# Row sums taken from VectorE to GpSimd, and copies set ahead of exponentials in the last slots, in an attention block with top-32 masking

## The reference

```python
x = x + attn(layernorm(x)); x = x + ffn(layernorm(x))
# attn:
scores = q @ k.T * SCALE + (q @ rel_k[dist])           # dist clipped to +-64
threshold = top_k(scores, 32)[0][..., -1:]
attn = softmax(where(scores < threshold, -inf, scores))
for i in range(3):                                      # v_curr = v at first
    a_v = attn @ v_curr
    if i == 0: a_v = a_v + attn applied to rel_v[dist]
    v_curr = a_v
    res = res + sigmoid(alphas_raw)[i] * v_curr
out = res @ Wout.T + bout
# ffn: x @ base_w.T + base_b, plus 8 low-rank experts weighted by a softmax gate
```

## Time and profile before

| | |
|---|---|
| median of 3 runs | 712.65 us |
| profiled execution, own time | 714.7 us |
| its span, first to last instruction | 713.0 us |
| DVE, PE, ACT, POOL busy, share of span | 95%, 93%, 87%, 77% |
| granted TensorE clock, mean | 0.98 |
| a slot without batch work | 10.07 us, two heads of 5.03 |

### The profile page before, as it was taken

The page is one execution under the profiler, slowest core; times in us unless marked ns, Lnnn a source line. Parts: engine busy times, 40 slices in busy tenths (PEclk is TensorE's granted clock), DMA queues, the critical chain, the costliest instruction groups (busy, mean ns, idle before and its releaser), DMA issues.

```text
span 713.0 us, 20948 instructions
## 1 busy us (share of the span) xinstructions
PE 659.8 (93%) x5780; PEld 512.2 (72%) x5780; DVE 679.7 (95%) x2820; ACT 618.9 (87%) x1767; POOL 547.0 (77%) x978
## 2 busy tenths in 40 slices
PE   4368999999999999999999999999999999999796
PEld 3256777777777777777787777777777777777574
DVE  6899999999999999999999999999999999999953
ACT  4578899989999899989999899998999899998753
POOL 1588888778878788878877788778878788787840
PEclk9769999999999999999999999999999999999998
DMA  6745545544454454544454545454545454445212
GB/s 197 176 127 139 148 124 163 161 126 144 142 155 133 132 154 130 157 142 143 133 155 128 156 137 153 123 158 129 153 135 161 133 146 136 140 146 151 70 44 59
DMA packets 148338, 98.72 MB, mean 138 GB/s; under 512 B 10624, under 2 KB 147968, under 8 KB 148096
## 3 DMA queue, kind: packets, MB, share of 16 engines
q1 hardware_dynamic: 147920, 97.32, 47.2%
q10 hardware_dynamic: 304, 0.08, 0.0%
HBM read 45.59 MB, written 51.77 MB: 137 GB/s over the span
## 4 chain that ended last, share of the span: by engine, by line
DVE 77%; issue 9%; PE 5%; POOL 4%; DMA 2%; ACT 2%; SPq 0%; ACTq 0%; DVEq 0%; POOLq 0%
DVE top L722 40%; DVE work L728 34%; POOL s_sb L330 2%; DMA band_scratch<-zeros 1%; PE ps_p L947 1%; DVE rinv L709 1%; ACT a_sb L477 1%; PE ps_y L967 1%; POOL xn L372 1%; DMA band_scratch<-band 1%; DVE stats L744 0%; DMA skew<-band_scratch 0%; DVE xn L798 0%; DVE x_sb L737 0%; POOL wk L351 0%
## 5 line engine op out<-in xcount | busy, mean ns | idle before, releaser
L722 DVE MAX8 top<-work 128x8 f32<-128x256 f32 x768 | 285.6, 415 | 0.0
L728 DVE MATCH_REPLACE8 work<-top,work 128x256 f32<-128x256 f32 x512 | 206.5, 413 | 0.0
L330 POOL TENSOR_TENSOR s_sb<-s_sb,pen 128x512 f32<-128x512 f32 x127 | 161.9, 1275 | 39.5 <-ACT pen L467 38.3
L335 POOL TENSOR_SCALAR a_sb<-a_sb,rinv 128x256 f32<-128x256 f32 x254 | 118.7, 478 | 55.2 <-DVE rinv L709 54.8
L477 ACT ACTIVATE a_sb<-s_sb,nmax 128x256 f32<-128x256 f32 x256 | 128.2, 501 | 34.9 <-POOL s_sb L330 26.9
L467 ACT ACTIVATE pen<-s_sb,limit 128x256 f32<-128x256 f32 x254 | 116.4, 511 | 24.2 <-POOL limit L317 24.0
L305 POOL TENSOR_TENSOR s_sb<-s_sb,skew 128x384 f32<-128x384 f32 x128 | 128.3, 1003 | 4.3 <-DMA skew<-band_scratch 4.3
L947 PE MATMUL ps_p<-aT,rows 128*64 128x256 f32 x1024 | 125.3, 386 | 1.3 <-issue 0.5
L728 DVE MATCH_REPLACE8 work<-top,s_sb 128x256 f32<-128x256 f32 x256 | 103.2, 412 | 0.0
L722 DVE MAX8 top<-s_sb 128x8 f32<-128x256 f32 x256 | 94.7, 413 | 5.0 <-POOL s_sb L305 5.0
L855 PE MATMUL ps_a<-ident,a_sb 128*128 128x128 f32 x512 | 84.9, 289 | 13.8 <-POOL a_sb L335 13.8
(11 more groups left out here) (166 smaller groups left out, 1310.7 us busy)
## 6 DMA issues: line engine op xcount, KB each, us to landing
skew<-band_scratch SPq DMA_DIRECT2D x128, 192.0 KB, 2.7
diag_scratch<-a_sb SPq DMA_DIRECT2D x128, 192.0 KB, 3.1
band_scratch<-band SPq DMA_DIRECT2D x128, 191.0 KB, 3.7
diag<-diag_scratch SPq DMA_DIRECT2D x128, 128.0 KB, 2.2
wqkv<-in_wqkv SPq DMA_DIRECT2D x1, 1152.0 KB, 8.3
x_sb<-in_x SPq DMA_DIRECT2D x4, 256.0 KB, 4.7
wout<-in_wout SPq DMA_DIRECT2D x1, 512.0 KB, 5.7
out<-xn SPq DMA_DIRECT2D x1, 512.0 KB, 3.3
```

What stands on the lines that cost most here:

```text
L330: nc.gpsimd.tensor_tensor(s_sb[g % 4][:], s_sb[g % 4][:], pen[g % 2][:], ALU.subtract).then_inc(pen_added, 1)
L335: nc.gpsimd.tensor_scalar(a_sb[g % 3][:, t, :], a_sb[g % 3][:, t, :], rinv[g % 2][:, t:t + 1], 1.0, ALU.mult, ALU.mult).then_inc(normed, 1)
L722: nc.vector.max(m[:, t, 8 * n:8 * n + 8], src).then_inc(top_step, 1)
L728: nc.vector.match_replace(work[t][:, n % 2, :], m[:, t, 8 * n:8 * n + 8], src, LOW).then_inc(top_step, 1)
```

## The change

- `add_projection` leaves VectorE for the seven batches of the loop. ScalarE copies `ps_y` into a new SBUF tile `yp_sb` at the end of slots q = 11, 19, ..., 59 (`save_projection`), and GpSimd adds that tile to x in the next slot, between `negative_max(2q+1)` and `add_penalty(2q)`. The row moments stay on VectorE and move behind the second head of that slot. The last batch's add in the tail stays as it was.
- `second_normal` is split: one tile in slots with q % 8 = 7, the other in the slot after it. The transposes, layer products and their copies move one slot back with it.
- In slot 63 GpSimd's `add_penalty(126)` comes ahead of shift and normalised tiles.
- In slots 61, 62 and 63 (`late`) `save_diagonals` stands ahead of `exponent(2q-1)`, `save_aT(2q-1)` and `save_values` ahead of `exponent(2q)` on ScalarE, and TensorE does `diagonal_columns` ahead of `attention_columns(2q-2)`.
- In the tail VectorE does the last gate's small steps between and behind the sums of the first output group, and the second group's sums after them.

```diff
+        yp_sb = sb("yp_sb", [P, T, DIM])
...
-            def second_normal(b):
+            def second_shift(b):
                 i = slice(T * b, T * (b + 1))
                 pool.wait_ge(rstd2_done, b + 1)
                 nc.gpsimd.tensor_tensor(shift[:, i], shift[:, i], rstd[:, i], ALU.mult).then_inc(shift_done, 1)
+
+            def second_normal(b, t):
+                i = T * b + t
                 pool.wait_ge(shift_done, b + 1)
...
+                nc.gpsimd.tensor_scalar(yn[:, i, :], y_sb[:, i, :], rstd[:, i:i + 1], shift[:, i:i + 1], ALU.mult,
+                                        ALU.add).then_inc(yn_done, 1)
...
                 if b >= 0 and q % NP == 7:
-                    second_normal(b)
+                    second_shift(b)
+                    second_normal(b, 0)
+                if b >= 1 and q % NP == 0:
+                    second_normal(b - 1, 1)
+
+            def add_projection(b):
+                i = slice(T * b, T * (b + 1))
+                pool.wait_ge(yp_saved, b + 1)
+                nc.gpsimd.tensor_tensor(y_sb[:, i, :], y_sb[:, i, :], yp_sb[:], ALU.add).then_inc(y_done, 1)
...
+                if q >= NP + 4 and q % NP == 4:
+                    add_projection(q // NP - 1)
                 second_steps(q)
...
+            add_penalty(2 * q)
             second_steps(q)
-            add_penalty(2 * q)
+            second_normal(INSIDE, 1)
...
+            def save_projection(b):
+                act.wait_ge(proj_done, NP * (b + 1))
+                reach(act, y_done, b)
+                nc.scalar.copy(yp_sb[:].rearrange("p t d -> p (t d)"), ps_y[:, 0:T * DIM]).then_inc(yp_saved, 1)
...
+                late = not on(q + 3)
+                if late:
+                    save_diagonals(q - 2)
                 if on(q - 1):
                     exponent(2 * q - 1)
                     save_aT(2 * q - 2)
-                if on(q - 2):
+                if on(q - 2) and not late:
                     save_diagonals(q - 2)
...
                 second_steps(q)
+                if late:
+                    save_aT(2 * q - 1)
+                    save_values(q - 1)
                 if on(q):
                     exponent(2 * q)
...
+                if q >= NP + 3 and q % NP == 3:
+                    save_projection(q // NP - 1)
...
-                if g % 2 == 0 and q >= NP + 4 and q % NP == 4:
-                    add_projection(q // NP - 1)
+                if g % 2 == 1 and q >= NP + 4 and q % NP == 4:
                     row_moments(q // NP - 1)
...
-            send_rows(0, 0, 4)
+            send_rows(0, 0, 4, (0,))
             dve.wait_ge(last_f, T)
             last = ps_p1[:, 0:T * REST].rearrange("p (t c) -> p t c", t=T)
             gate_logits(DONE, TILES, last[:, :, 0:E_])
+            send_rows(0, 0, 4, (1,))
+            low_rank(1, DONE, TILES, last[:, :, E_:REST])
             send_rows(1, 4, B - 1)
-            low_rank(1, DONE, TILES, last[:, :, E_:REST])
             send_rows(2, B - 1, B)
...
-                            reach(pe, y_done, b)
+                            reach(pe, yp_saved, b)
```

More of the change, by code:

```diff
@@ L159, in preln_attention_ffn @@
         rows_ready, rows_saved = sem("rows_ready"), sem("rows_saved")
-        proj_done, y_done, var2_done = sem("proj_done"), sem("y_done"), sem("var2_done")
+        proj_done, yp_saved, y_done, var2_done = sem("proj_done"), sem("yp_saved"), sem("y_done"), sem("var2_done")
         rstd2_done, shift_done, yn_done = sem("rstd2_done"), sem("shift_done"), sem("yn_done")
@@ L369, in second_normal @@
                 nc.gpsimd.tensor_tensor(shift[:, i], shift[:, i], rstd[:, i], ALU.mult).then_inc(shift_done, 1)
+            def second_normal(b, t):
+                i = T * b + t
                 pool.wait_ge(shift_done, b + 1)
-                for i in range(T * b, T * (b + 1)):
-                    nc.gpsimd.tensor_scalar(yn[:, i, :], y_sb[:, i, :], rstd[:, i:i + 1], shift[:, i:i + 1], ALU.mult,
-                                            ALU.add).then_inc(yn_done, 1)
+                nc.gpsimd.tensor_scalar(yn[:, i, :], y_sb[:, i, :], rstd[:, i:i + 1], shift[:, i:i + 1], ALU.mult,
+                                        ALU.add).then_inc(yn_done, 1)
             def second_steps(q):
@@ L559, in second_steps @@
                 b = q // NP - 2
-                if 0 <= b < INSIDE and q % NP == 0:
+                if 0 <= b < INSIDE and q % NP == 1:
                     save_ynT(b)
-                if 0 <= b < INSIDE and q % NP in (1, 2):
-                    save_layer(b, q % NP - 1)
+                if 0 <= b < INSIDE and q % NP in (2, 3):
+                    save_layer(b, q % NP - 2)
+            def save_projection(b):
+                act.wait_ge(proj_done, NP * (b + 1))
+                reach(act, y_done, b)
+                nc.scalar.copy(yp_sb[:].rearrange("p t d -> p (t d)"), ps_y[:, 0:T * DIM]).then_inc(yp_saved, 1)
             def slot(q):
@@ L587, in slot @@
                 second_steps(q)
+                if late:
+                    save_aT(2 * q - 1)
+                    save_values(q - 1)
                 if on(q):
                     exponent(2 * q)
-                if on(q - 1):
+                if on(q - 1) and not late:
                     save_aT(2 * q - 1)
@@ L791, in low_rank, with send_rows @@
                                         middle.unsqueeze(2).to_broadcast([P, n, E_, R_]), ALU.mult).then_inc(z_done, 1)
-            def send_rows(i, a, e):
+            def send_rows(i, a, e, tiles=range(T)):
                 dve.wait_ge(by_done, (2, 3, 4)[i])
-                for t in range(T):
+                for t in tiles:
                     dve.wait_ge(l_ready, T * i + t + 1)
@@ L1016, in second_steps @@
                 b = q // NP - 2
-                if 0 <= b < INSIDE and q % NP == 0:
+                if 0 <= b < INSIDE and q % NP == 1:
                     second_columns(b)
-                if 0 <= b < INSIDE and q % NP in (1, 2):
-                    layer(b, q % NP - 1)
+                if 0 <= b < INSIDE and q % NP in (2, 3):
+                    layer(b, q % NP - 2)
             def slot(q):
@@ L1029, in slot @@
                     scores(q + 1)
+                late = not on(q + 3)
+                if late:
+                    diagonal_columns(q - 2)
                 if on(q - 1):
                     attention_columns(2 * q - 2)
-                if on(q - 2):
+                if on(q - 2) and not late:
                     diagonal_columns(q - 2)
```

## The result

The changed kernel takes 708.74 us (median of 7 runs, 706.78 to 709.58), the kernel before, beside it, 713.2 us (7 runs, 711.84 to 714.18). The ratio is 0.9936, with an interval of 0.9921 to 0.9951: faster, by 0.6%. The forecast was 708.1 us with a range of 706.5 to 710.4, and 4.5 us less than before; the medians differ by 4.5. The profiled execution took 707.67 us, its span is 705.7 us.

A forecast was written before the change was run, and what follows sets the result against it. VectorE was taken to bound the loop. The terms -3.15 + 0.7 - 1.0 + 0.2 - 0.8 - 0.45 = -4.5 us took the median of 712.65 us to 708.1 us, range 706.5 to 710.4.

The forecast's parts named there:

- What bounds the kernel: Loop: VectorE works 558.73 of 560 us; work taken off it is time, work elsewhere free unless VectorE is kept waiting.
- The sum off VectorE: Loop: moving the sum off VectorE saves 0.45 us, seven times, 3.15 us.
- GpSimd's sum at 0.73, hidden by 0.82 us: Loop: GpSimd's sum takes 0.73 us like clip and fits, with nothing left, into 0.82 us free ahead of the penalty.
- New waits: Loop: ScalarE's copies and GpSimd's sum add 0.1 us of waiting per batch, 0.7 us; bounds 0 and 2.6.
- The wait in slots with q % 8 = 7: Six slots before slot 63: splitting the normalised tiles removes the division's wait, 6 x 0.17 = 1.0 us.
- The late slots: Slots 61 and 62 lose 0.1 us each, together 0.2, bounds 0 and 0.6; in slot 63 two effects cancel.
- The tail start: Start of tail: with v copied earlier, TensorE's products start 0.8 us sooner; bounds 0.3 and 1.1.
- The end: Last gate's sum starts 0.5 us earlier; second group's transfer 1.3 us later may hold the last; gain 0.45, bounds 0 and 0.8.
- Half given back: Loop: GpSimd's sum at 1.152 us, or combined delays, cost 0.37 us a batch; 710.0 us; chance 14%.
- all given back: Loop: GpSimd's sum comes back whole on the path, 4.4 us more; 712.5 us, no change; chance 5%.
- a slow sum: Loop: GpSimd's sum takes far longer than clip beside the searches; at 1.9 us, 715.1 us, slower; chance 3%.
- The tail that doesn't move: Tail: diagonals or TensorE's order hold it, last transfers queue; 0.8 and 0.45 us missing; 709.4 us; chance 12%.

The follow-up runs named there:

- the doubled sum: Changed kernel with a second GpSimd sum of the same size, into a tile nobody reads, ahead of the real one: 710.71 us, ratio 0.9973.
- sum-only kernel: Kernel before with only the copy on ScalarE, the sum on GpSimd and the moments behind the odd head: 709.72 us, ratio 0.9955.
- old-end experiment: Changed kernel with the last gate again behind all sums of the first output group: 708.12 us, ratio 0.9921.
- the run again: Changed kernel unaltered, timed and profiled once more beside the kernel before: 708.48 us, ratio 0.9924.
- two outputs by tile: Changed kernel with first and second output groups each sent in two transfers, and the late order in slot 63 alone: 708.67 us, ratio 0.9918.
- sum back: Changed kernel with the projected rows added by VectorE again, without ScalarE's copy and GpSimd's sum: 711.27 us, ratio 0.9962.

## Why the prediction was right, step by step

- **What bounds the kernel.** It held. What was taken from VectorE in the loop came out as time, and the two other engines took theirs at no cost that shows.
- **The sum off VectorE, forecast 3.15 us.** Measured 0.44 to 0.47 a batch by two experiments, seven times 3.1 to 3.3 us.
- **GpSimd's sum at 0.73, hidden by 0.82 us.** The sum takes 0.731 us (726 to 738 ns), as clip does in the earlier trace rows. GpSimd takes 0.731 / 0.41 = 1.8 times VectorE's time for it, and still it costs nothing. The Trainium skill (GPSIMD Engine Reference, Engine selection) keeps such sums on VectorE because GpSimd is about twice as slow; the trace agrees with the ratio, but the move gained 0.46 us a batch, as long as the time fits into GpSimd's gap. With the sum doubled the overhang came back at once, 0.49 us a batch.
- **New waits, forecast 0.7 us, measured 0.** This term was mis-sized, for two reasons. I set the copy's 0.27 us, a duration less its overlap, against the 0.19 us of waiting in the earlier trace rows, and so found it 0.1 us too long. But a wait also takes away the overlap of its neighbours, so that the room is wider than the idle time shown: the step from the rows copy to the ramp is 0.77 us without the copy and 0.77 with it, and the copy's own step is 0.29 (631.81 - 631.52). And GpSimd's sum fits with 0.18 us to spare, not "with nothing left": 0.68 us after its start at 637.15, as behind the doubled sum (642.04 - 641.36), the penalty could have followed, at 637.83, and it started at 638.01, behind the ramp. The slack itself, 0.05 us at even heads, was read rightly: behind the doubled sum 0.52 us of delay cost 0.49. Odd heads have 0.25 us, before and after, which no experiment used up.
- **The wait in slots with q % 8 = 7, forecast 1.0 us, measured 6 x 0.27 = 1.6.** Mechanism right, size off: I counted the idle time shown, 0.17, and left out the overlap of 0.08 to 0.10 that a wait destroys. It is the error of the copy over again, and both made the forecast gain too small.
- **The late slots, forecast 0.2 us in slots 61 and 62, nothing in slot 63.** Measured 0.27 for three slots, 0.09 in each, and 0.27 gained in slot 63, where the wait at head 126 went with the earlier penalty: together 0. The 14 heads from 112 to 126 show the sum of it: 71.85, less 0.46 for the sum, less 0.27 for that wait, and 0.27 more for the late heads, is 71.39.
- **The tail start, forecast 0.8 us, measured 0.72.** Of it 0.56 come from the order of copies, the other 0.16 remain without that order and are those of the earlier penalty (2.55 in the sum-only kernel, 2.39 here). What held the products was not the landing of the diagonals: the last fetch was issued at 669.68 and landed 2.2 us later, at 671.88. TensorE's diagonals (672.19) waited for the rows copy, which stands behind head 126's exponentials and ends at 671.43 + 0.61 = 672.04. The transposes of head 126 started at 672.85, when TensorE was through with the diagonals (672.82) and GpSimd with the normalisation (671.86 + 0.93 = 672.79); no run separates these two.
- **The end, forecast 0.45 us, measured 0.28** between before and after, 0.2 by the old-end experiment. VectorE's part was right: the gate's sum comes 29.71 us behind division 126 before, 28.44 after, 1.27 less, of which 0.72 are the tail start and 0.55 this term's 0.5. What I had named as a bound was the fact, and the term was too large by it: the second group's transfer is issued 1.3 us later (7.22 us behind the projection's sum instead of 5.93) and now sets the end in place of the last sum. Counted from the last transfer's issue at 702.90, the 2.25 us of before would have ended the span at 705.15; it ended at 705.7.
- **The sum.** With the measured terms it is -3.2 + 0 - 1.6 + 0 - 0.72 - 0.28 = -5.8 us; the pieces of the traces gave 5.7. The forecast of 4.5 was too small by this, by 0.7 us of waits that didn't come, 0.6 us of a wait that was worth more than it shows and 0.2 us of late heads that were paid back, less some 0.2 us of tail and end. The medians say 4.5 us, with the interval from 3.5 to 5.6 (713.2 times what is missing to 1), and in the second series 713.76 - 708.48 = 5.3, with the interval from 3.9 to 6.9. So the mechanism and the signs were right, and that the first medians give the forecast to the digit is luck.
- **The rivals.** Half given back, all given back, and a slow sum are refuted by the absent waits and by 731 ns. The tail that doesn't move is refuted for its start and true in part for the end.

The times can't decide between 4.5 and 5.7 us: the latter lies just outside the first interval and inside the second. The start varies by up to 3 us from one execution to the next, together with its waits, and what makes those vary was not followed.

## What to carry to other kernels

Where one engine works without a gap, the price of an edit is read as the gap on the other engines at that very place, between the instruction ahead and the one that is waited for: a sum that GpSimd does 1.8 times as slowly was free in 0.8 us of room, and a second one wasn't. The slack of one place isn't that of another: odd and even heads differ by 0.17 us. A wait is wider than the idle time that the profile shows, by the lost overlap with its neighbour. On the bounding engine it costs that much more (0.25 to 0.27 us for 0.17 shown), and on another engine it holds that much more work (a copy with a step of 0.29 us in 0.19 shown). At the end of a kernel ask which transfer or sum ends last, and what the edit makes later there, before moving instructions; and compare pieces between repeating instructions, since a start that varies by 3 us hides 0.3 us of work.

## What was not expected of the hardware

**A single store of a diagonal can land far later than its neighbours.** In the profiled execution of the changed kernel the store sent at 140.03 took 5.1 us to land, while those from 150 to 650 us take 2.0 to 4.4 with a median of 2.2. The fetch of this diagonal is issued when the store has landed, at 145.10, and lands at 147.40. SyncE's issue and its landing, and the TensorE row that used the diagonal:

```profile
L238 SPq DMA_DIRECT2D diag_scratch<-a_sb x1: 459/459/459, 140.0 to 140.0; - x1
...
DMA to landing us min/median/max: 5.1/5.1/5.1
```

```profile
147.45 0.63 PE L942 MATMUL ps_d<-ident,diag 128*128 128x128 f32 x4 [0.87 <-issue]
```

TensorE idles 0.87 us, the diagonal's copies and the exponentials follow, and the division of head 24 waits 0.45 us. In the run again it didn't come. Single waits of the division behind the start stand in three other kernels. Those of 0.67 us (sum only, head 18) and of 0.41 and 1.86 us (two outputs by tile, heads 44 and 50) show the same picture, with TensorE idle for 1.06, 1.0 and 1.8 us ahead of its diagonals; the cause of one of 0.24 us (sum back, head 68) was not followed. No run ties them to an edit.

**TensorE's granted clock at the end depends on the execution.** Of its two levels 1.00 is the full one, 2.4 GHz, and 0.50 the lower, 1.2 GHz. The mean is 1.00 from 700 to 702 us and 0.73 from 702 to 704 in the changed kernel, and the last products at 701.79 and 702.01 take 0.37 and 0.27 us. In the run again, with everything some 1 us later, it is 0.98 and then 0.50, and the same products take 0.58 and 0.42. In both TensorE had waited 1.62 us for VectorE shortly before, ahead of its product at 701.10 and at 702.10:

```profile
700.00:702.00 2.00, 0.48 (x4) 0.29 (x3) 1.78 (x8) 0.49 (x2) 0.72 (x1) 0.98 0.03 9
702.00:704.00 2.00, 1.27 (x5) 0.69 (x5) 1.14 (x4) 0.28 (x1) 0.00 (x0) 0.50 0.97 258
...
702.94 0.58 PE L1091 MATMUL ps_y<-lorab,zT 64*128 64x128 f32 x1 [0.37 <-ACT zT L629]
...
703.31 0.42 PE L1091 MATMUL ps_y<-lorab,zT 64*128 64x128 f32 x1
```

The last sum comes 0.45 us later with it (8.06 against 7.61 us behind the projection's), and yet the end is 10.92 us in both: from the last sum's start to the end it is 2.86 us instead of 3.31. The second group's transfer, issued 7.22 us behind the projection's sum in both, sets the end, whatever the clock.
